# Attention scores as two column tiles: one product per head instead of one per pair of heads

## The reference, cut to what matters

```python
def _gqa(q, k, v):                       # 16 query heads in 8 groups of 2, head width 128
    scale = 1.0 / np.sqrt(q.shape[-1])
    scores = jnp.einsum('bsghd,btgd->bghst', q, k) * scale
    p = jax.nn.softmax(scores, axis=-1)
    return jnp.einsum('bghst,btgd->bsghd', p, v)
...
core = _gqa(q, k, v)                     # over the sequence itself
xout = _gqa(qx, kx, vx)                  # over the context, also 64 long
```

## Time and profile before

| | |
|---|---|
| time of three runs | 983.66, 979.86, 983.66 us; median 983.66 |
| span of the profiled execution, first to last instruction | 978.1 us |
| what lies around the span, taken against the median | 5.6 us |
| scores: TensorE records (L372) | 1024 loads, 1024 passes, from 36.9 to 657.3 us |
| busy share of the span | PE 97%, DVE 82%, ACT 75%, POOL 47% |
| chain that ended last | PE 82%, of it b_sc L372 10% |

### The profile page before, as it was taken

One profiled execution on the slowest core, in us unless ns is written; L12 is line 12 of the kernel. 1 busy time (PEld: TensorE's weight loads), 2 busy tenths in 40 slices (PEclk: granted clock), 3 DMA queues, 4 the chain that ended last, 5 costly groups with the idle time before them and its releaser, 6 DMA issues.

```text
span 978.1 us, 21551 instructions
## 1 busy us (share of the span) xinstructions
PE 946.2 (97%) x7240; PEld 674.7 (69%) x7240; DVE 798.2 (82%) x1720; ACT 736.5 (75%) x1370; POOL 458.5 (47%) x673
## 2 busy tenths in 40 slices
PE   5699999999999999999999999999999999999997
PEld 2476777777777777777777777776655566666665
DVE  6889999999999999999999999989799754444443
ACT  6988888888888888888888888865556645555554
POOL 5335655455465555555564655541036703333333
PEclk9999999999999999999999999999999999999999
DMA  9924201010001000100100010211558733343223
GB/s 220 330 73 87 44 23 55 23 47 26 28 29 45 28 28 23 49 29 22 50 23 28 28 45 28 72 65 55 182 166 241 232 114 50 50 70 57 44 29 38
DMA packets 36747, 70.35 MB, mean 72 GB/s; under 512 B 3617, under 2 KB 24737, under 8 KB 36513
## 3 DMA queue, kind: packets, MB, share of 16 engines
q1 hardware_dynamic: 27184, 54.39, 17.6%
q0 software_dynamic: 9456, 14.59, 8.8%
HBM read 55.52 MB, written 18.68 MB: 76 GB/s over the span
## 4 chain that ended last, share of the span: by engine, by line
PE 82%; DVE 9%; ACT 4%; issue 2%; POOL 1%; DMA 1%; POOLq 0%; DVEq 0%; ACTq 0%
PE b_pj L346 23%; PE b_sc L372 10%; PE b_tr L362 8%; PE b_o L401 7%; PE b_acc L444 5%; PE b_pj L1337 5%; PE b_o L1372 5%; PE b_o L1464 3%; PE b_pt L391 3%; PE b_tr L1337 3%; PE b_sc L1337 3%; PE b_pj L1417 2%; PE b_pt L1361 2%; PE b_sc L1417 1%; PE b_tr L1417 1%
## 5 line engine op out<-in xcount | busy, mean ns | idle before, releaser
L698 POOL TENSOR_TENSOR root<-vareps,neghalf 128x4 f32<-128x4 f32 (+1 forms) x128 | 174.2, 1361 | 10.0
L691 POOL TENSOR_TENSOR var<-ssq,unit 128x4 f32<-128x4 f32 (+1 forms) x128 | 54.4, 425 | 253.4 <-DVE ssq L524 253.4
L346 PE MATMUL b_pj<-w_hi,xq 128*128 128x512 f16 x384 | 147.9, 385 | 1.1 <-DVE xq L680 0.9
L346 PE MATMUL b_pj<-w_lo,xq 128*128 128x512 f16 x384 | 147.5, 384 | 0.0
L456 ACT ACTIVATE sq<-b_pj 128x512 f32<-128x512 f32 x192 | 114.9, 598 | 38.0 <-PE b_pj L346 35.0
L524 DVE TENSOR_REDUCE ssq<-sq 128x4 f32<-128x512 f32 x192 | 130.2, 678 | 9.4 <-ACT sq L456 9.4
L535 DVE TENSOR_TENSOR nrm<-raw,rstd 128x512 f32<-128x512 f32 x192 | 128.3, 668 | 1.6 <-POOL rstd L702 1.2
L372 PEld LDWEIGHTS b_sc<-kT,qT 128*128 128x128 f32 x1024 | 121.7, 192 | 6.1 <-ACT qT L483 1.7
L1313 POOL DMA_INDIRECT out<-xn x39 | 60.6, 1554 | 133.5 <-ACT xn L1543 124.0
L372 PE MATMUL b_sc<-kT,qT 128*128 128x64 f32 x1024 | 122.5, 273 | 0.7 <-ACT qT L483 0.7
L362 PE MATMUL b_tr<-ident,nrm 128*128 128x128 f32 x768 | 116.4, 274 | 6.8 <-DVE nrm L535 3.6
(11 more groups left out here) (327 smaller groups left out, 2271.7 us busy)
## 6 DMA issues: line engine op xcount, KB each, us to landing
nst<-in_ffw SPq DMA_DIRECT2D x40, 512.0 KB, 3.7
wload<-in_ffw SPq DMA_DIRECT2D x20, 512.0 KB, 4.5
xbuf<-zero SPq DMA_DIRECT2D x13, 387.0 KB, 9.7
xn<-xbuf SPq DMA_DIRECT2D x9, 516.0 KB, 3.7
x_sb<-in_x SPq DMA_DIRECT2D x4, 512.0 KB, 13.8
wproj<-in_ctxT SPq DMA_DIRECT2D x1, 2048.0 KB, 10.3
xhl<-in_w_all SPq DMA_DIRECT2D x4, 512.0 KB, 17.4
wproj<-in_wprojT POOLq DMA_DIRECT2D x4, 512.0 KB, 6.3
```

What stands on the lines that cost most here:

```text
L346: last = pe.matmul(o, x, w[kind][:, k, at:at + BANK], start=(k == 0 and n_ == 0), stop=(k == KT - 1 and n_ == len(terms) - 1))
L698: pool.tensor_tensor(root[:, r % 2, c, :], vareps[:, r % 2, c, :], neghalf[:, 0:1].unsqueeze(2).to_broadcast(shape), ALU.pow).then_inc(s[" ...
```

## The change

The loop over b gets a loop over the two heads h inside. Each product now takes 64 stationary columns (one head's tokens) and writes 64 partitions of b_sc, those of its head: h = 0 to partitions 0 to 63, h = 1 to 64 to 127. A product whose output starts at partition 64 uses the right half of the array's columns, one that starts at 0 the left half, so the two are two column tiles. The moving operand is the same kT columns for both. Results land where they landed before, and nothing else of the kernel is changed; the semaphore is still raised once, by the last product of the slot.

```diff
                 for g in range(GU):
                     for b in range(2):
-                        last = pe.matmul(b_sc[:, (g * 2 + b) * S:(g * 2 + b + 1) * S], qT[:, r % 2, g * 2 + b, :],
-                                         kT[:, r % 2, g, b * S:(b + 1) * S], start=True, stop=True)
+                        for h in range(HPG):
+                            rows = slice(h * S, (h + 1) * S)
+                            last = pe.matmul(b_sc[rows, (g * 2 + b) * S:(g * 2 + b + 1) * S], qT[:, r % 2, g * 2 + b, rows],
+                                             kT[:, r % 2, g, b * S:(b + 1) * S], start=True, stop=True)
                 last.then_inc(s["sc_done"], 1)
```

## The result

| | before | after |
|---|---|---|
| median of the runs | 981.76 us (4 runs) | 956.21 us (4 runs, 955.5 to 956.7) |
| ratio | | 0.9739, 95% interval 0.9716 to 0.9762 |
| span of the profiled execution | 978.1 us | 954.5 us |
| one round of four slots | 38.36 us | 36.57 us |

The kernel is 25.6 us faster by the medians and 23.6 by the spans; 957 was forecast. An execution of the changed kernel with a span of 954.5 us took 956.3, so some 1.8 us lie around the span, not the 5.6 of the prediction; the profiled execution of before was one of the quicker ones.

The account below looks back on a forecast made before the run. TensorE was taken to bound attention; its 0.56 us less a slot shrinks to 0.46 as DVE becomes next, and 60 x 0.46 = 27 us off 983.7 gives 957 us. Range 946 to 973, or 946 to 999 to reach 0.8.

Parts of the forecast that it names:

- The bound: Attention rounds of four slots: TensorE busy for all 38.36 us, so it sets the pace; DVE has 2.62 us to give.
- The load as the burst's limit: Old score burst: each product streams 53 of 112 ns and waits for its load of 128 float32 columns, 107 ns.
- The step of a pair, 58 ns: Tiled score burst: two heads' passes side by side take 53 + 5 = 58 ns, the burst 0.93 us.
- The burst of before, 1.79 us: Old score burst: 16 records 0.112 us apart, 1.79 us; the chain books 1.73 because one step falls to a neighbour.
- The mode's price, 0.30 us: TensorE entering and leaving tiled mode around each score burst: 0.30 us once a burst, bounds 0.19 and 0.35.
- What is late next: After the change DVE sets the pace: 35.74 us of work plus 0.79 of waits, 36.53 us a round.
- How many slots: Attention slots: 56 at full gain and eight at the ends at half, as 60, each 0.46 us, 27 us in all.
- The range: Whole kernel: 946 to 973 us for the likeliest case, its best end 945; 946 to 999 to reach 0.8.
- A: Rival, score burst: the array's two halves do not work side by side; 18 us slower, 1002 us; chance 0.18.
- B: Rival, score burst: tiles overlap only in part, if only neighbours do; 975 to 984 us; with C, 0.09 for a gain.
- C: Rival, TensorE's clock: new gaps bring it down now and then, leaving 974 us; chance 0.09 together with B's gain.

Follow-up runs that it names:

- lighter vector engine: Kernel before the change without DVE's rounding of the quantized attention output: 981.67 us (0.9983); the same cut in the changed kernel: 953.77 us (0.9705).
- short stream: Kernel before the change with each score product's moving operand cut from 64 to 32 columns in all slots but the first: 983.62 us, one run.
- one head first: Changed kernel with a slot's sixteen score products reordered, all eight of head 0, then all eight of head 1: 993.33 us (1.0114).
- pairs of two: Changed kernel with score products reordered, for each group both sequences of head 0, then both of head 1: 957.52 us (0.9751).

## Why the prediction was right, step by step

- **The bound.** Right. TensorE alone set the pace: neither a lighter vector engine nor fewer streamed columns moved the round from 38.36 us.
- **The load as the burst's limit.** Right, shown by the short stream.
- **The step of a pair, 58 ns.** Right: 0.058 us, taken from the row tiles, whose rows were the only ones of two tiles at work. Two column tiles share the array's rows and overlap all the same. The rule of the Trainium skill's page "TensorE: Matmul & The Clock Gate" (section "The mechanism"), that a load overlaps passes in flight only if its row group is another one, doesn't hold here: even one tile alone takes 58 ns for a load and a pass that the prediction puts at 53 each. (The section also lets a load run ahead into a background weight buffer; no run here tells which place a load went to.) The 1.59x estimated from its section "Measured speedup vs the span model" was too low: 1.79 us of steps became 0.93, 1.9x.
- **The burst of before, 1.79 us.** Too long by 0.06 in three slots of four: it is 1.73, and the step that the prediction has fall to a neighbour doesn't. TensorE had 2.07 us a round to give, not 2.24.
- **The mode's price, 0.30 us.** Right in sum: 0.09 us on the way in, 0.05 for the first step, 0.10 on the way out and 0.05 to 0.06 within the transposes behind, on top of 16 steps of 0.058: 1.23 us, as summed.
- **What is late next.** The number was right, 36.53 us a round forecast and 36.57 measured, the reason was not. I had said that DVE becomes full and that its waits for squares and exponentials stay, 0.79 us a round. They vanished (ssq from 7.5 to 0.3 us), the wait for y stayed in part, a wait for rstd came, and DVE's work can be cut without effect. DVE's share is 97% (35.38 of 36.57), not 98%, and its waits did not set the round. What is missing from 2.24 us is 0.17 that the bursts never had, and 0.30 at one set of transposes that wait for DVE's norm product, a step and not a full engine. That the two sums agree is luck.
- **How many slots.** 58 slots from the sixth burst on gained 24.9 us, 0.43 each; I had 60 at 0.46. With the 1.3 us given back outside, that makes 23.6 us on the spans for the 27 of the forecast. That 957 is still met within a microsecond is luck too: the forecast started from 983.66, a time with the longer opening of before, and 3.7 us of that opening are in none of the changed kernel's times. They were most of the 5.6 us that the prediction adds around the span.
- **The range.** By its own sum the best end is 983.7 - 39 = 945 us, not 946; nothing hangs on it.
- **Rivals.** A is real but needs the other order, and its steps are 58 ns, not 56. B did not happen: a pass goes ahead of up to three others. C neither, the granted clock is 1.00 throughout the rounds.

## What to carry to other kernels

When passes stream fewer columns than their loads bring in, look at whether the recorded pass is longer than its columns explain (275 ns here for a stream worth 219): then the load is the bound, and splitting the stationary side into column tiles halves it (1.79 us of steps to 0.93), if products of different tiles stand within three passes of each other. Order within the burst decides the sign: the same sixteen products cost 956 us alternating and 993 us one head after the other. And before moving a step to the front of an in-order queue because someone waits for it, look at what it waits for itself; the work that stood ahead of it may have been its cover.

## What the runs showed of the hardware that was not expected

- TensorE, said above to run its instructions in order, does not start the passes of two column tiles in the order of the program: a pass for an idle tile goes ahead of up to three that haven't started (one head first, 416.43 us; pairs of two, 320.63). Within one tile they keep their order as far as the starts show. With the heads alternating a burst takes 0.93 us, with pairs of two 0.98, with one head first 1.68.
- Four column tiles issue 64 loads and 64 passes in 0.88 us, 14 ns for each pair of them; the 25 ns between the router's small products are no floor for tiles.
- DVE's busy time is no measure of its need: with the same 74 instructions a round it was busy 35.74 us in a round of 38.36 and 35.38 in one of 36.57. Back to back its instructions start 0.60 us apart and are recorded with 0.68, so a wait behind an instruction adds the last 0.08 to the busy time.
